# The last batch of edge states in two parts, and a new order of the steps that fix and gather states

## The reference, cut to what matters

```python
# graph: N = 6250 nodes, E = 206250 edges sorted by target node (dst)
def gat_conv(x, W, a_src, a_dst, bias, src, dst):
    src, dst = with_self_loops(src, dst)
    xw = (x @ W).reshape(N, 8, 16)
    e = leaky_relu(sum(xw * a_src)[src] + sum(xw * a_dst)[dst], 0.2)
    m = segment_max(e, dst)
    p = exp(e - m[dst])
    alpha = p / segment_sum(p, dst)[dst]
    return segment_sum(xw[src] * alpha, dst).reshape(N, 128) + bias
row, col = edge_index
h0 = gat_conv(layernorm(x), W0, ..., row, col)            # conv1: all edges
nr, nc = row[col], col[col]                               # conv2: its edges use only the first N edges
h1 = gat_conv(layernorm(x), W1, ..., with_loops(nr, nc))
x = x + layernorm(concat(h0, h1) + layernorm(x)) * gamma + beta
# then 8 experts, 2 per node, chosen by a gate: h = gelu(y @ W1[e] + b1[e]) @ W2[e] + b2[e]
```

## Time and profile before

| | |
|---|---|
| median of 3 runs | 3386.95 us (3384.83 to 3387.03) |
| profiled execution | 3386.33 us, its span 3384.2 us |
| VectorE, ScalarE busy | 1849.6, 1199.8 us |
| GpSimd busy | 2083.5 us, 1522.3 of it issuing the gathers of line 668 |
| TensorE busy | 956.0 us |
| median us to landing: gather of line 668, store of a batch | 2.6, 8.8 |

### The profile page before, as it was taken

One profiled execution on the slowest core, in us unless ns is written; L12 is line 12 of the kernel. 1 busy time (PEld: TensorE's weight loads), 2 busy tenths in 40 slices (PEclk: granted clock), 3 DMA queues, 4 the chain that ended last, 5 costly groups with the idle time before them and its releaser, 6 DMA issues.

```text
span 3384.2 us, 28080 instructions
## 1 busy us (share of the span) xinstructions
PE 956.0 (28%) x6022; PEld 872.9 (26%) x6023; DVE 1849.6 (55%) x3386; ACT 1199.8 (35%) x2081; POOL 2083.5 (62%) x2086
## 2 busy tenths in 40 slices
PE   4600000000000000000000000000444999999998
PEld 2400000000000000000000000000334999999997
DVE  8446666656555665556655556656773433433433
ACT  3323444334333334333343333331452333333332
POOL 5677777777777777777777777775674222222222
PEclk8755555555555555555555555555555999999999
DMA  9734454433443433443334433368555222222222
GB/s 292 149 81 119 137 162 156 133 116 117 124 139 116 117 117 116 143 120 117 116 116 131 132 117 116 116 149 138 158 177 184 36 36 36 36 37 36 37 36 31
DMA packets 210558, 384.32 MB, mean 114 GB/s; under 512 B 69023, under 2 KB 164787, under 8 KB 203449
## 3 DMA queue, kind: packets, MB, share of 16 engines
q0 software_dynamic: 80224, 157.28, 22.6%
q1 hardware_dynamic: 129145, 225.88, 19.9%
q10 hardware_dynamic: 1120, 0.52, 0.1%
HBM read 198.41 MB, written 185.17 MB: 113 GB/s over the span
## 4 chain that ended last, share of the span: by engine, by line
POOL 48%; PE 25%; issue 16%; DVE 6%; DMA 2%; ACT 1%; DVEq 1%; SPq 0%; POOLq 0%; ACTq 0%
POOL AR L668 45%; PE ps L1065 11%; PE ps L1071 10%; POOL AR L656 1%; DVE AR L1154 1%; POOL adstart L640 1%; PE ps L1033 1%; ACT AR L923 1%; PE ps L1045 1%; PE ps L1056 1%; PE ps L1024 1%; DVE group_stats L1450 0%; DVE AR L1573 0%; DVE AR L1571 0%; DMA state<-AR 0%
## 5 line engine op out<-in xcount | busy, mean ns | idle before, releaser
L668 POOL DMA_INDIRECT AR<-tables,idx x1612 | 1522.3, 944 | 491.3 <-issue 491.3
L1009 PE MATMUL ps<-ident,sml 128*128 128x128 f32 x4 | 1.6, 501 | 2129.7 <-DVE sml L1367 2129.7
L748 POOL DMA_INDIRECT out<-AR,idb x105 | 191.8, 1827 | 584.8 <-issue 552.6
L1009 PEld LDWEIGHTS ps<-ident,sml 128*128 128x128 f32 x4 | 1.0, 310 | 2130.2 <-DVE sml L1367 2130.2
L1300 DVE TENSOR_TENSOR_SCAN AR<-ps,AR 128x512 f32<-128x512 f32 (+1 forms) x486 | 518.8, 1141 | 4.0
L1267 DVE TENSOR_TENSOR AR<-AR,ps 128x248 f32<-128x248 f32 (+1 forms) x54 | 30.5, 566 | 744.9 <-DMA AR<-tables,idx 744.9
L853 ACT COPY AR<-AR 128x1984 f32<-128x1984 f32 (+1 forms) x108 | 421.8, 3954 | 0.7 <-DVE AR L1300 0.7
L847 ACT ACTIVATE ps<-AR 128x512 f32<-128x512 f32 x432 | 254.2, 596 | 466.2 <-DVE AR L1300 466.2
L1065 PEld LDWEIGHTS ps<-AR 128*128 128x128 f32 x3360 | 392.9, 192 | 6.5 <-DVE AR L1658 1.2
L1065 PE MATMUL ps<-AR 128*128 128x128 f32 x3360 | 393.5, 276 | 0.8 <-DVE AR L1658 0.8
L1294 DVE TENSOR_TENSOR AR<-AR,ps 128x3968 f32<-128x3968 f32 (+1 forms) x54 | 366.0, 6777 | 0.2
(11 more groups left out here) (287 smaller groups left out, 1804.1 us busy)
## 6 DMA issues: line engine op xcount, KB each, us to landing
state<-AR SPq DMA_DIRECT2D x53, 2232.0 KB, 8.8
AR<-tables,idx POOLq DMA_INDIRECT x1661, 2.6
AR<-in_L_ffn_W SPq DMA_DIRECT2D x16, 1024.0 KB, 9.2
AR<-placed SPq DMA_DIRECT2D x105, 129.0 KB, 2.1
AR<-adstart SPq DMA_DIRECT2D x53, 248.0 KB, 3.3
adstart<-zero SPq DMA_DIRECT2D x26, 496.0 KB, 5.1
tables<-AR SPq DMA_DIRECT2D x49, 136.0 KB, 2.9
hbd<-eb2b SPq DMA_DIRECT2D x7, 896.0 KB, 7.1
```

Of the source, the lines that this page charges most:

```text
L668: pool.indirect_dma_start(out=G[s][:, j, 0:ROWT], out_offset=None, in_=table_rows, in_offset=bass.IndirectOffsetOnAxis(ap=idx[:, s, j:j + ...
L748: pool.indirect_dma_start(out=out, out_offset=bass.IndirectOffsetOnAxis(ap=idb[:, s, :], axis=0), in_=ys[:, s, :], in_offset=None, bounds_ ...
```

## The change

The last batch is processed in parts of 16 (`CUT`) and 15 columns, each packed with 17 places to a feature (`VIEW[17]`), so that scans and decays have 17/32 of their elements. The gathers of columns 17 to 31 count on another semaphore (`conv2_gathered`), so VectorE's first part waits for 16 columns alone. The carry goes through the tile `carry` from the one packing to the other. SyncE stores each part when its copies are done. On VectorE `fix_sums(1)` stands before `combine(1, 2)`, and `shares(1, 4)` and `combine(1, 4)` move into the turn of group 0. On GpSimd `last_states1(0)` stands directly behind the wait for the stored fixed rows, ahead of `last_states2(4)`, and `last_states1(1)` and `last_states2(6)` change as the diff shows.

```diff
+CUT = 16
@@ addresses
+        VIEW = {}
+        for w in (L, CUT + 1):
+            n = HD * w
+            flat = {"Z": cut(1152, n), "W": cut(1152 + HL, n), "R": cut(1152 + 2 * HL, n), "M": ps[2][:, 0:n], "N": ps[2][:, HL:HL + n], "E": ps[3][:, 0:n],
...
@@ SyncE, fetch_and_store
+                    if b == NB - 1:
+                        at_ = b * J * ROWS
+                        sp.dma_start(states0[:, at_:at_ + CUT * ROWS], G[0][:, 0:CUT, :].rearrange("p j r -> p (j r)")).then_inc(batch_stored[0], 16)
+                        sp.wait_ge(rows_copied, b + 4)
+                        sp.dma_start(states0[:, at_ + CUT * ROWS:at_ + J * ROWS], G[0][:, CUT:J, :].rearrange("p j r -> p (j r)")).then_inc(batch_stored[0], 16)
+                        return
@@ GpSimd
-            gather(0)
+            for j in range(J):
+                pool.indirect_dma_start(out=G[0][:, j, 0:ROWT], out_offset=None, in_=table_rows,
+                                        in_offset=bass.IndirectOffsetOnAxis(ap=idx[:, 0, j:j + 1], axis=0)).then_inc(batch_gathered[0] if j < CUT else conv2_gathered, 16)
@@ GpSimd, after last_states2(0 to 2), the fix rows' load, last_states2(3)
             store_fix_rows(1, 0)
+            pool.wait_ge(fix_rows_stored, 32)
+            last_states1(0)
             last_states2(4)
-            pool.wait_ge(fix_rows_stored, 32)
-            for n in range(2):
-                last_states1(n)
-                last_states2(5 + n)
+            last_states2(5)
+            last_states1(1)
+            last_states2(6)
             for n in range(2, 4):
                 last_states1(n)
@@ ScalarE
-            for b in range(NB):
-                whole_batch(b % NS, b // NS, b, b < NB - 1)
+            for b in range(NB - 1):
+                whole_batch(b % NS, b // NS, b, b < NB - 2)
+            w = CUT + 1
+            batch_weights(NB + 1, CUT, False, w)
+            turn_part(1, CUT, J)
+            batch_decays(NB + 1, w)
+            copy_back(NB + 1, 0, CUT, 0, w)
+            batch_weights(NB + 2, J - CUT, False, w)
+            batch_decays(NB + 2, w)
+            copy_back(NB + 2, 0, J - CUT, CUT, w)
...
-            for g in range(2, 5):
+            for g in range(2, 4):
                 share_exps(1, g)
...
+                if g == 0:
+                    share_exps(1, 4)
@@ VectorE
+            b, w = NB - 1, CUT + 1
+            V.memset(VIEW[w]["M"][1][:, :, 0], 0.0)
+            V.memset(VIEW[w]["R"][1][:, :, 0], -BIG)
+            dd()
+            marks(b + 2, 0, CUT, same[:, b * J:b * J + CUT], w=w, next_w=w)
+            dve.wait_ge(batch_gathered[0], 16 * (BS * J + CUT - J))
+            scan_batch(b + 2, 0, CUT, w=w, next_w=w)
+            marks(b + 3, 1, J - CUT, same[:, b * J + CUT:C], True, w=w)
+            dve.wait_ge(conv2_gathered, 16 * (J1 + J - CUT))
+            scan_batch(b + 3, 0, J - CUT, at_=CUT, w=w, next_w=w)
+            V.tensor_copy(carry[:, :], VIEW[w]["T"][1][:, :, J - CUT])
...
             fix_maxima(1)
             shares(1, 2)
+            fix_sums(1)
             combine(1, 2)
-            fix_sums(1)
             shares(1, 3)
-            shares(1, 4)
             combine(1, 3)
-            combine(1, 4)
...
```

More of the change, by code:

```diff
@@ L829, in turn_first_adst, with batch_weights @@
                 S.copy(AI[s][:, :, 1], chunk_adst[:, k, k * HD:(k + 1) * HD]).then_inc(adst_turned, 1)
-            def batch_weights(q, n, conv2):
+            def batch_weights(q, n, conv2, w=L):
+                W, WP, TS = (VIEW[w][k][1] for k in ("W", "WP", "T"))
                 hold(act, 2, weight_diffs_ready, q + 1)
@@ L1280, in scan_batch @@
                     hold(dve, 4, rows_copied, q)
+                if w != L and at_ == 0:
+                    V.tensor_copy(TS[:, :, 0], carry[:, :])
                 V.tensor_copy(TS[:, ROWT:ROWS, js], RM[:, :, js])
-                V.tensor_copy(Z[:, :, 0], RM[:, :, n])
+                if next_w != w:
+                    dd()
+                V.tensor_copy(VIEW[next_w]["Z"][1][:, :, 0], RM[:, :, n])
                 dd()
@@ L1436, in _ @@
             dd()
-            for b in range(2, NB):
+            for b in range(2, NB - 1):
                 if b < PEEL:
                     add_biases(b - 2)
-                whole_batch(b % NS, b // NS, b, b == NB - 1)
+                whole_batch(b % NS, b // NS, b, CUT + 1 if b == NB - 2 else L)
                 if b == FIX:
@@ L1600, in _ @@
                     choose(g - 1)
+                if g == 0:
+                    shares(1, 4)
                 if g + 1 < NG:
@@ L1606, in _ @@
                     settle(g - 1)
+                if g == 0:
+                    combine(1, 4)
                 if g < 2:
```

58 lines of the change are left out of this document (36 added, 22 removed).

## The result

The changed kernel takes 3394.24 us (median of 12 runs, 3392.01 to 3395.77); the kernel before takes 3386.85 us on the same chip (12 runs, 3384.64 to 3388.42). The ratio is 1.0023, 95% interval 1.0014 to 1.0032: slower by 7.4 us, just beyond the 0.2% that this measurement tells from no change. The profiled execution took 3394.40 us, its span 3392.3 us, against 3386.33 and 3384.2.

What follows compares the result with a forecast made beforehand. Full DMA queues of slow conv2 gathers, then GpSimd's issue of 28 gathers, were taken to bound the stretch. Restart +0.7 and regrouping +3.0 gave +3.7 on 3386.33: 3390.0 us, range 3385 to 3393.5 (0.55), eight in ten 3376 to 3397.

Steps and rivals of the forecast that it cites:

- rival 1: SP's loads after combine(1,2) take turns with gathers and fix store: restart at 2323, +9 us, total 3396; chance 0.21.
- The split's own times: Last batch on VectorE: part 1 hidden under gathers, part 2's scans 5.6 us, second store issued at 2273.6, 11.4 us earlier.
- Store 2 stands behind the gathers issued up to 2273 and lands near 2292: DMA queue after the last batch: second state store, 1.1 MB, served in issue order, landing near 2292 instead of 2299.0.
- store 1: First state store of the last batch, 1.18 MB, issued at 2256.6: pushes every later conv2 gather back by 3.4 us.
- the fourth group: Conv2 gathers ahead of the fix store in GpSimd's queue: same work in another order, done at 2316 to 2316.5.
- Fix begun at 2300.4: VectorE's fixing of the loaded rows, after combine(1,1): begins at about 2300.4 instead of 2305.30.
- Fix store lands at 2317: GpSimd's store of the fixed rows: issued at 2304.0 but landing at about 2317, behind the fourth conv2 group.
- the early sums: Fix sums before combine(1,2) on VectorE: fix store issued 11.3 us earlier, all of it lost in the DMA queue.
- Restart +0.7: GpSimd going on to state gathers after the fix store lands: at 2317.3 instead of 2316.58, +0.7 us.
- 28 gathers, 40.3 us to shares(0,1): GpSimd's gathers between restart and shares(0,1): bound by issue, 38.3 us as before, so shares(0,1) starts at 2357.6.
- Regrouping +3.0: Group 4 moved into VectorE's loop: 14.4 us from shares(0,1) to conclude(0) instead of 11.31, net +3.0 us.
- Rival 2: DMA between last batch and fix store: slow gathers overlap with stores, -16 us, total 3370.5, half 3378; chance 0.24.

Runs made afterwards that it cites:

- e7: The changed kernel with combine(1,4) put back ahead of the shares of conv1 group 1: +4.9 us against the kernel before, ratio 1.0015.
- e12: The kernel before with fix_sums(1) ahead of combine(1,2), and nodes without a conv2 edge gathering their own row: -5.6 us against the kernel before, ratio 0.9983.
- e1: The kernel before with the change's new order of all engines, the last batch left whole: +1.2 us against the kernel before, ratio 1.0003.
- e3: The kernel before, with nodes without a conv2 edge gathering their own row instead of one common row: -2.3 us against the kernel before, ratio 0.9995.

## Why the prediction was right or wrong

The forecast was 3390.0, +3.7 us. The measured 3394.24, +7.4 us, lies in the range of eight in ten (3376 to 3397), but outside the 3385 to 3393.5 that the forecast's own mechanism was given with 0.55. Slower beyond 0.2% had 0.21, and the result is slower by 0.23%, nearer to the 3396 of rival 1. Step by step:

*The split's own times: right.* Scans at 17 to a feature 5.36 us (5.6 predicted), product 3.41 (3.4), part 1 wholly under the gathers, second store issued at 2273.29 (2273.6).

*"Store 2 stands behind the gathers issued up to 2273 and lands near 2292": the step that failed.* It landed at 2303.45. The prediction took from one place, the store of 2285.00, that transfers are served in order of issue, and priced the queue as a sum of parts that cost the same in any order ("the same work in another order ends at the same time"). In the changed kernel two of the gathers issued after the store landed before it. The 21 gathers were done at 2307.2, where the rows gave 2293.4 + 6.6 (2.29 MB at 347 GB/s) = 2300.0, and the same bytes took 8.2 us more than before, 7.7 of them in the packets of the gathers. So there are two losses: the store does not keep its place ahead of later gathers, and the mixed work costs more than its parts. It begins with store 1: priced at 3.4 us, it goes with a landing of the second group's last gather that is 6.5 us later (2270.67 + 18.2 = 2288.9, was 2282.4). And the fourth group, which was to be in at 2316 to 2316.5, was in at 2321.8 (2312.44 + 9.4). The Trainium skill, "DMA: Bandwidth & Descriptors", section "Queues, rings and completion order", has each DMA engine take turns between queues, packet by packet. This trace agrees with it from 2288 on (79 to 106 GB/s with both at work) and not from 2278.6 to 2288 (46 GB/s with store 2 issued and waiting), as the trace before did not at 2285 (45 GB/s, then 347). The rule by itself does not account for the 8.2 us.

*Fix begun at 2300.4: 2310.42. Fix store 3.6 us behind it: right,* 3.40. *Fix store lands at 2317: 2322.0,* after 8.2 us, so the gain of the early sums was indeed lost in the queue, as said. *Restart +0.7: +5.7.* This is the term that was mis-sized, by 5.0 us. The point that the prediction gave for rival 1, a restart later than 2320, was passed; the place of its loss was another. It had SP's loads after 2309 cut in before the fix store. In fact these loads were issued at 2319.04, 5.2 us behind the fix store, and the state stores had already delayed the fix load by 4.4 us. So part of the agreement is luck: the rival's restart came by a loss that nobody had priced.

*28 gathers, 40.3 us to shares(0,1): right,* 39.3. *Regrouping +3.0: +2.55,* and e7 shows that this combine is on the path. Together +5.7 - 1.0 + 2.55 = +7.3 at conclude(0), where +3.7 was forecast; another 0.8 comes behind it.

*Rival 2, the backlog doesn't bind:* it fell on the first chip, where the engines are full through the whole stretch (share 0.95 to 1.11 from 2273 to 2304) and the fix store lands at 2322.0, not at 2306 to 2308.

*Not foreseen:* that the same change costs 10 us on other chips by another road. There VectorE waits on issue for 42 us instead of 23, and 6 us of it reach the fix. The prediction priced the second copy of the batch's code at 0.1 to 0.3 us for memsets and copies, and its instructions at nothing; on the first chip that holds (0.2 us of such waits).

*What stays open.* On the first chip the cause is read from two traces, not tested. The equal bytes by queue rule out that more was moved, but why the gathers' packets take longer beside a store is not shown. No later run met a chip like it, so whether keeping the stores apart from the gathers, or own rows, gives the 5 us back there was not seen. That e12 is faster there is likewise not shown. And what VectorE waits for on the other chips is not in the profile: that it is the delivery of its instructions is argued from where the waits lie (straight code that runs once, more of it with the split, longer in some places after less idle time), not shown. Two readings speak for caution. The profile's queue of instructions has the same 60 packets, 0.49 MB, in the kernel before and the changed one on the first chip and in the changed kernel and e12 on the other. And there the profile puts much of ScalarE's idle time in the main loop on issue too, over 1000 us in e12, which in the kernel before on the first chip are waits for VectorE; so "issue" can hide a releaser on those chips.

## What to carry to other kernels

Work that is taken off an engine in front of a store may only move the store into whatever stands in the DMA queues then: look where the transfer will land, not where it is issued, and bound it for both ways of service, by order and in turns. When a loop's last pass is written out in parts, that can cost time of its own, and it may not show on the chip that was profiled. And before reordering around a full queue, ask what fills it: here three lines that spread one repeated gather index, with one call moved, gained 5.6 us on a chip where the split and the new order together lost 10.0.

## What the runs showed of the hardware

- Gathers of one common row: 14 of them, each 128 rows x 576 B, took 0.61 of the DMA engines' time over 21 us (e1); with own rows 0.16 (e3), at the same 46 to 49 GB/s.
- The same bytes (1.9 MB of gathers, 5.3 MB of stores and loads) took the engines 45.0 us with one store behind the gathers and 53.2 us with two stores among them, on the first chip; SyncE's packets took 15.4 us in both, the gathers' 30.7 and 38.4.
- The kernel before ran at 3387 us on the first chip and at 3660, 3669, 3668 and 3675 us on four others. In the changed kernel one gather of the main loop takes GpSimd 1055 ns on average in a slower one (1581 of them) where the first chip took 944: 1581 x 0.111 = 175 us of the difference of some 280. It is not every gather: the medians are 949 and 944 ns, the longest 1953 and 1532. First the slower chip, then the first one:

```profile
L682 POOL DMA_INDIRECT AR<-tables,idx x1581 | 1667.8, 1055 | 524.4 <-issue 510.2
```

```profile
L682 POOL DMA_INDIRECT AR<-tables,idx x1581 | 1493.2, 944 | 481.9 <-issue 481.9
```

- On the slower chips VectorE's waits on issue end 0.70 us or a multiple of it apart (in e12 at 2526.07, 2527.48, 2531.69, 2533.07, 2535.87, 2538.68, 2541.47: steps of 1.41, 4.21, 1.38, 2.80, 2.81, 2.79), and they go on while the DMA engines are idle. They are not confined to the last batch: from 300 to 2200 us e12 has 192 us of them, the kernel before on the first chip 2.0. DMA share in tenths and GB/s in 40 slices of the changed kernel from 2543 to 2562 us, in which VectorE waits 7.9, 1.2 and 3.3 us on issue:

```profile
DMA  0000000000000000000000000000000000000000
GB/s 0 0 0 0 0 0 0 0 0 0 0 0 0 0 0 0 0 0 0 0 0 0 0 0 0 0 0 0 0 0 0 0 17 0 0 0 0 0 0 0
```

  The Trainium skill, "Runtime: NRT & Kernel Launch", section "Instruction fetch mechanics", has engines stream straight code from memory ahead of execution, at a cost that is mostly hidden; if these waits are that, the trace does not agree: 42 us in a stretch of 77 are not hidden.
